# The loop over pairs of token groups written out as straight code, with constant counts in all waits

## The reference

```python
q, k = exp(split(x @ Wq.T + bq)), exp(split(x @ Wk.T + bk)); v = split(x @ Wv.T + bv)
kv = cumsum(k[..., :, None] * v[..., None, :], axis=1); k1 = cumsum(k, axis=1)
attn = einsum('zsD,zsDd->zsd', q, kv) / sum(q * k1, -1)
x1 = layernorm(x + merge(attn) @ Wo.T + bo)
scores = sigmoid(x1 @ gate_w.T)             # 8 experts of the 2 best of 4 groups, by scores + bias
w = 2.5 * scores[top8] / sum(scores[top8])
y = sum_e w_e * down_e(silu(gate_e(x1)) * up_e(x1)) + shared(x1)
out = layernorm(x1 + y)
```

## Time and profile before

| | before |
|---|---|
| median of 3 runs | 566.63 us (564.98 to 568.44) |
| profiled execution, its own time | 563.56 us |
| span of the profiled execution | 561.8 us |
| mean granted TensorE clock | 0.947 |
| PE, DVE, ACT, POOL busy | 84%, 70%, 47%, 49% of the span |
| instruction records | 11711 |

### The profile page before, as it was taken

One profiled execution on the slowest core, in us unless ns is written; L12 is line 12 of the kernel. 1 busy time (PEld: TensorE's weight loads), 2 busy tenths in 40 slices (PEclk: granted clock), 3 DMA queues, 4 the chain that ended last, 5 costly groups with the idle time before them and its releaser, 6 DMA issues.

```text
span 561.8 us, 11711 instructions
## 1 busy us (share of the span) xinstructions
PE 472.9 (84%) x3994; PEld 364.4 (65%) x3994; DVE 394.2 (70%) x931; ACT 265.4 (47%) x451; POOL 274.5 (49%) x200
## 2 busy tenths in 40 slices
PE   5576399969989897969999896969999799878992
PEld 2564388747766686747766685757867577646771
DVE  1335547787787868787787766787697768876754
ACT  3604324763349333763349332573348534625451
POOL 2525015653456524663456523653357525755682
PEclk9776679999999999999999997998999999989998
DMA  7200183306153345407053345214353161507430
GB/s 266 105 1 2 31 181 73 79 1 158 19 132 76 82 95 121 90 1 165 11 132 75 82 95 124 67 21 101 76 129 77 31 146 53 114 9 149 95 76 19
DMA packets 28603, 47.15 MB, mean 84 GB/s; under 512 B 1920, under 2 KB 10368, under 8 KB 28160
## 3 DMA queue, kind: packets, MB, share of 16 engines
q1 hardware_dynamic: 28544, 46.36, 34.9%
HBM read 43.73 MB, written 2.62 MB: 83 GB/s over the span
## 4 chain that ended last, share of the span: by engine, by line
PE 26%; issue 25%; POOL 19%; DVE 14%; ACT 3%; DMA 3%; POOLq 1%; DVEq 0%; SPq 0%; ACTq 0%
PE bank L278 24%; POOL units L813 9%; POOL hidden_lo L846 4%; DVE hidden_lo L614 3%; DMA weight_wide<-weight_d 2%; DVE units L724 2%; POOL rstd L832 2%; POOL k_sum L842 1%; DVE stats L634 1%; ACT units L515 1%; ACT hidden_hi L496 1%; POOL x_lo L837 1%; DVE exp_neg L667 1%; DVE x L646 1%; PE bank L467 1%
## 5 line engine op out<-in xcount | busy, mean ns | idle before, releaser
L813 POOL TENSOR_TENSOR units<-units,weight_wide 128x512 f32<-128x512 f32 x128 | 174.3, 1368 | 223.3 <-DVE units L724 223.3
L515 ACT ACTIVATE units<-bank 128x512 f32<-128x512 f32 x136 | 81.2, 597 | 158.4 <-PE bank L278 81.9
L724 DVE TENSOR_TENSOR units<-bank,units 128x512 f32<-128x512 f32 x136 | 93.2, 685 | 46.2 <-ACT units L515 32.5
L614 DVE TENSOR_TENSOR hidden_lo<-units,hidden_hi 128x512 fp32r<-128x512 f32 x112 | 93.9, 838 | 31.0 <-ACT hidden_hi L496 30.8
L496 ACT ACTIVATE hidden_hi<-units 128x512 fp32r<-128x512 f32 x136 | 85.4, 628 | 58.3 <-POOL units L813 44.6
L278 PE MATMUL bank<-hidden_hi,down_hi 128*128 128x512 f32 x136 | 59.1, 434 | 30.3 <-POOL hidden_lo L846 18.0
L278 PE MATMUL bank<-x_hi,gate_hi 128*128 128x512 f32 x136 | 64.5, 474 | 16.8 <-DVE units L724 9.3
L278 PEld LDWEIGHTS bank<-hidden_hi,down_hi 128*128 128x128 f32 x136 | 25.8, 190 | 49.8 <-POOL hidden_lo L846 25.5
L278 PE MATMUL bank<-x_hi,up_hi 128*128 128x512 f32 x136 | 54.9, 403 | 1.0 <-ACT units L515 1.0
L624 DVE TENSOR_TENSOR probs<-bank,const 128x512 f32<-128x512 f32 x64 | 41.2, 685 | 19.9 <-PE bank L278 19.9
L278 PE MATMUL bank<-x_lo,gate_hi 128*128 128x512 f32 x136 | 54.7, 402 | 0.0
(11 more groups left out here) (97 smaller groups left out, 751.7 us busy)
## 6 DMA issues: line engine op xcount, KB each, us to landing
weight_wide<-weight_d SPq DMA_DIRECT2D x64, 512.0 KB, 6.7
xT<-xT_in SPq DMA_DIRECT2D x8, 512.0 KB, 5.9
x_tok<-x_in SPq DMA_DIRECT2D x8, 256.0 KB, 7.5
out_dram<-out_sb SPq DMA_DIRECT2D x8, 256.0 KB, 2.3
weight_wide<-up_in SPq DMA_DIRECT2D x1, 1088.0 KB, 9.2
up_raw<-up_in SPq DMA_DIRECT2D x1, 1088.0 KB, 11.3
down_raw<-down_in SPq DMA_DIRECT2D x1, 1088.0 KB, 13.5
weight_d<-weightT SPq DMA_DIRECT2D x8, 64.0 KB, 1.8
```

The source lines that it names most:

```text
L515: nc.scalar.activation(units[n % 3][:, :], up_banks[2 * n % 3][:, :], ACT.Silu).then_inc(silu_done, 1)
L614: V.tensor_tensor(hidden_lo[n % 3][:, :], units[n % 3][:, :], hidden_hi[n % 3][:, :].bitcast(F32), ALU.subtract).then_inc(hidden_lo_done, 1)
L724: V.tensor_tensor(units[n % 3][:, :], up_banks[(2 * n + 1) % 3][:, :], units[n % 3][:, :], ALU.mult).then_inc(gated_done, 1)
L813: G.tensor_tensor(units[n % 3][:, :], units[n % 3][:, :], weight_wide[:, (n - 1) % (2 * PIECE), :], ALU.mult).then_inc(hidden_done, 1)
```

## The change

The loop is taken away on all five engines. A Python loop issues the same slots of groups 0 to 5 one after another in the same order, so that g is a plain number throughout. Each wait then has a constant count and each DMA a constant address, and no engine has a counter or a jump. The parity u is as before. Where g is the plain number 0, the waits meant for it come into force in the rest of group 0 as well: SyncE waits for `gate_split` ahead of two of its loads.

```diff
-            with eng.Fori(0, (GROUPS - 2) // 2) as pair:
-                for u in range(2):
-                    g = pair * 2 + u
-                    run(rest, g, u, ffn=True, mid=True, front=True, tail=False)
-                    run(head, g + 1, 1 - u, ffn=True, mid=True, front=True, tail=True)
+            for g in range(GROUPS - 2):
+                u = g % 2
+                run(rest, g, u, ffn=True, mid=True, front=True, tail=False)
+                run(head, g + 1, 1 - u, ffn=True, mid=True, front=True, tail=True)
```

## The result

| | before | after |
|---|---|---|
| median (4 runs each) | 566.83 us (564.98 to 568.44) | 553.19 us (552.50 to 553.62) |
| profiled execution, own time | 563.56 us | 553.34 us |
| its span | 561.8 us | 551.6 us |
| mean granted TensorE clock | 0.947 | 0.946 |
| instruction records | 11711 | 10732 |

The ratio is 0.9759, with a 95% interval of 0.9728 to 0.9791: faster by 2.4%. 553.5 was predicted, with 549.5 to 558.5 as range. Four single runs of the last series count as slow and are left out of its ratios: 1532.59 us (both edits of experiment 8), 1127.75 us (after, once more) and 567.40 and 568.00 us (before).

A forecast was written before the change was run, and what follows sets the result against it. TensorE was taken to bound the kernel, with two loop jumps stalling it. Five stretches fall from 318.12 to 306.34 us, saving 11.8: 551.8 by profile, 554.8 by median, so 553.5 us, range 549.5 to 558.5.

The forecast's parts named there:

- Bound and place: TensorE bounds the six stretches (slot 5 to next group's slot 4); jumps cause its slot 5 gaps of 3.60 and 5.13 us.
- The rival that the gaps aren't the jump's: The stop between slots 4 and 5 stays in straight code; 565 to 567 us, no change; chance 0.04.
- First jump, 3.20 + 0.52 us: Stretch behind the first pass's end: 3.20 us of TensorE gap goes, plus 0.52 us from the late start further down.
- second, 4.73 + 1.82 + 1.75: Stretch behind the second pass's end, 8.30 us saved: 4.73 TensorE gap, 1.82 slower clock behind it, 1.75 further down.
- Further down is one thing I can name.: Jump excess beyond gap and clock: routing's exp_neg takes 1.26 us, not 0.23, beside a GpSimd multiply; TensorE waits 1.06 us.
- Granted clock 1.00 up to the end of stretch 5: Sign in the new profile: TensorE's granted clock is 1.00 from 90 us through the last of the six stretches.
- Register waits worth 0: Constant wait counts and DMA addresses on all five engines save 0, with 0.06 us loss in each of four stretches.
- the bound of 25 us: Upper bound on register savings: all TensorE gaps of a stretch, 5.0 us, times five.
- No stretch fell below 60.5: Sign: a stretch under 60.5 us in the new profile would show the register step wrong.
- Added code worth 0: Three code bodies for one cost 0 in fetches; TensorE's instruction queue keeps 4 blocks a stretch.
- Collision: exp_neg behind a GpSimd multiply: gone behind both jumps, kept in the first stretch; rival in every stretch 557.6 us, chance 0.15.
- 553.5 between 551.8 and 554.8: Forecast time in us, taken between the profiled execution's measure (551.8) and the median's (554.8).

The follow-up runs named there:

- experiment 8: Straight code with GpSimd's low part ahead of k_sum (552.11 us), TensorE's two high-part matmuls ahead of its wait (552.04 us), or both (552.53 us).
- after, once more: The changed straight-code kernel timed again, unaltered, in the last series: 553.47 us, ratio 0.9831 to before.
- experiment 1: Against the straight code, TensorE alone runs the loop of three passes, the other four engines stay straight: 561.75 us.
- experiment 7: Against the loop kernel, pass boundary moved from slot 5 to ahead of slot 14, two passes with one taken jump, groups 4 and 5 straight: 554.43 us.
- experiment 3: Against the straight code, VectorE alone runs the loop, the other four engines stay straight: 559.90 us.
- experiment 4: Against the straight code, wait counts of groups 0 to 5 come from a register on all engines but SyncE, without jumps: 553.45 us.
- experiment 2: Against the straight code, VectorE, ScalarE, GpSimd and SyncE run the loop, TensorE stays straight: 560.79 us.
- the kernel with short loops: Against the straight code, TensorE runs a tiny loop of four rounds ahead of slot 5 of groups 1 to 5: 556.83 us.
- the split wait: Against the straight code, TensorE issues the down product's two high-part matmuls ahead of its wait for the low part: 552.04 us.
- the hint: Against the loop kernel, a prefetch hint for the closing branch at the top of every pass, on all engines: 571.20 us.
- the low part first: Against the straight code, GpSimd does the low part of block 11 ahead of the k_sum product in slot 12: 552.11 us.

## Why the prediction was right, point by point

- **Bound and place.** Right. TensorE's two `issue` gaps at slot 5 were the jumps': they are gone in straight code and come back, at 3.0 us each, with TensorE's loop alone (experiment 1). The rival that the gaps aren't the jump's is out.
- **First jump, 3.20 + 0.52 us; second, 4.73 + 1.82 + 1.75.** As a difference of stretches the sum was right: 64.94 and 69.52 became 61.09 and 61.08, 12.29 us less where 64.94 + 69.52 - 2 x 61.28 = 11.90 was expected. As an account of causes it was incomplete. It took TensorE's gap for the whole jump. A gap isn't worth its length: in stretch 2 of experiment 1 the stop of 3.00 us made 3.85 us with a dip, so about 2.5 without, and in experiment 7 one of 2.71 us made nothing. The 0.52 us left over were thus a net of what is won back and of what the other engines add. VectorE's own jump costs 1.61 us by itself (experiment 3), and in before it lay beside TensorE's: TensorE alone 7.5 us over both stretches, all but TensorE 7.9, both together 12.0, each with its dips.
- **"Further down is one thing I can name."** Too simple for the second jump. Stretch 4 of before had a second stop with the lower clock behind it, which I had not looked for. Its slot 14, on TensorE, and the granted clock there in a cut of 6 us:

```profile
379.33 0.80 PE L278 MATMUL bank<-hidden_hi,down_hi 128*128 128x512 f32 x1 [2.21 <-POOL hidden_lo L846]
379.92 0.63 PE L278 MATMUL bank<-hidden_lo,down_hi 128*128 128x512 f32 x1
```

```profile
379.00:385.00 6.00, 5.67 (x24) 4.51 (x25) 4.28 (x9) 2.90 (x5) 3.30 (x4) 0.72 0.05 14
```

  With a dip of about 1.3 us there and the 0.52 of the first jump, the sum comes to 1.8 for the 1.75 us; no run took the two apart. The stop is not the jump's: every stretch has this stop of 2.2 us in both kernels.
- **Granted clock 1.00 up to the end of stretch 5.** Wrong, and the step that was mis-sized. I had put the lower clock down to the 4.49 us gap. It also falls behind the 2.2 us stop, in stretches 0, 1 and 5 of after, for 1.26 + 1.31 = 2.57 us in the stretches that I had summed. Against that stands a gain that I had at 0 (less 0.06): plain stretches of 61.09 in place of 61.28, which with 61.22 for the first is 306.34 - 5 x 61.09 = 0.89. So 10.10 us were saved for the 11.8 predicted: 11.78 - 2.57 + 0.89.
- **Register waits worth 0.** Right to 0.12 us a stretch (experiment 4); the bound of 25 us was nowhere near. No stretch fell below 60.5.
- **Added code worth 0.** Right: 4 blocks a stretch, and one `issue` wait of a matmul in the whole span, 1.01 us ahead of the six stretches (82.70). Experiment 7 shows that such a stop can be 1.48 us.
- **Collision.** Stretches 2 and 4 came to the good side as said. That stretch 0 would stay on the bad side was wrong: with constants it starts 0.01 us ahead of GpSimd's multiply (107.82 and 107.83), with registers behind it (experiment 4). Of its 0.60 us, 0.33 went although it has a clock dip now. So the collision was priced too low: with collision and dip stretch 0 took 63.03 us (experiment 2), with the dip alone 61.49, which makes it about 1.5 us. The 0.60 were that less the work that stretch 0 lacks.
- **553.5 between 551.8 and 554.8.** This was a choice, and it held, in part by luck. After's profiled execution took 553.34, 1.5 above the 551.8, mostly by the dips; and the 1.7 us that I put on top for the median weren't there. Two misses cancel. By the profiled pair the change is worth 10.2 us, by the medians 13.6, since before's profiled execution was 3.3 us faster than its median and after's is 0.15 slower. The guess that the jumps fluctuate has this for it: with the far jump at slot 5 on one or more engines the runs of a kernel scatter by 2.5 to 9.0 us (9.0 in the 17 runs of before in the last series), after by 1.1 in 4 and 2.2 in 5 runs. Against it, the kernel with short loops scatters by 5.6 us as well, and of the 4.6 us by which the two jumps of before differ, about 1.3 are the dip in slot 14. The single runs were not traced, so it stays a guess. The dips scatter too: of the runs with the split wait, three with a mean clock of 0.944 took 550.99 to 551.40, two with 0.938 took 552.67 and 553.65.

**What stays open.** That the far jump is dear because of its fetch is argued, not shown: fetched blocks and gap go together in each profile, each gap ends 1.3 to 2.0 us after a block has landed, register counts alone (experiment 4) bring no such gap and three near jumps together one of 1.5 us at most; but no run took the fetch away from a far jump. Nor is it known what decides whether the clock falls behind a stop: the same 2.2 us bring it in one stretch of six in before and in experiment 4, in three in after, in four with the hint. With the stop split it came in two (0.9 and 1.1 us, the low part first), in four (1.76 and 0.28, the split wait) and in four (1.57 and 0.5, both).

## What to carry to other kernels

A hardware loop whose body is long enough to be fetched anew cost TensorE and VectorE microseconds at each pass here; look for it as an `issue` gap behind the pass's end on the engine that sets the pace, and as a late first instruction on another, where it can hide under the name of a third. Write the loop out where code size allows, or put the pass's end where the pacing engine waits anyway, which here hid TensorE's stop of 2.71 us wholly. And before a gap's cost is taken as gone, look behind every other stop of the same engine for the lower clock: shorter stops elsewhere may be answered by dips that eat the gain.

## What the runs showed that I had not expected

- TensorE's clock went to the lower level behind a stop of 2.2 us, in about half of the cases, at 1.26 to 1.31 us a time in after; shortening the stop to 1.76 us did not end it.
- VectorE's jump to the loop's start cost 1.3 us where TensorE's cost 2.7 to 4.5, and the profile named ScalarE for it.
- The hint on the loop made it slower by 0.8%.
- Straight code has `issue` stops of a matmul too, a few of 0.6 to 1.5 us, and each ends 1.3 to 1.5 us after a block of instructions has landed.
- A small VectorE step takes 0.23 or 1.26 us by whether it starts 0.01 us ahead of or 0.1 us behind a GpSimd multiply, and constants for registers in the waits were enough to change sides.
